# Adding the residual x to z with an accumulating DMA instead of GpSimd's additions

## What is computed

```python
y = jnp.einsum('bct,bcd->bdt', x, cond_w[condition])
z = jnp.einsum('bsd,od->bso', y, W) + b
u = jnp.einsum('bsd,edr->ebsr', y, A)
m = jnp.einsum('ebsr,ero,e->bso', u, B, p_scores)
gamma = jnp.minimum(0.5 * norm(z) / (norm(m) + 1e-6), 1.0)   # norms over the last axis
out = x + z + gamma * m
```

## Time and profile before

| | us |
|---|---|
| median of 3 runs | 942.87 |
| lowest and highest | 938.2 and 942.97 |
| the profiled execution: whole time | 940.29 |
| the profiled execution: span of instructions | 938.5 |
| granted clock of TensorE over the span | 0.990 of full speed |

### The profile page before, as it was taken

One profiled execution on the slowest core, in us unless ns is written; L12 is line 12 of the kernel. 1 busy time (PEld: TensorE's weight loads), 2 busy tenths in 40 slices (PEclk: granted clock), 3 DMA queues, 4 the chain that ended last, 5 costly groups with the idle time before them and its releaser, 6 DMA issues.

```text
span 938.5 us, 15150 instructions
## 1 busy us (share of the span) xinstructions
PE 914.9 (97%) x4884; PEld 789.7 (84%) x4884; DVE 576.1 (61%) x898; ACT 355.9 (38%) x694; POOL 317.9 (34%) x317
## 2 busy tenths in 40 slices
PE   6969999999999999999999999999999999999996
PEld 5858888888888888888888888888888888888885
DVE  4995555656555657555656555656556666556664
ACT  4443432433433443433343333343433343334342
POOL 0023323443323443224443224443224443224432
PEclk9989999999999999999999999999999999999999
DMA  7222112212112222122222122121122221122211
GB/s 258 84 75 89 47 70 92 92 70 92 45 71 92 87 75 86 42 78 92 78 84 78 41 87 92 70 92 69 46 92 92 70 92 65 50 92 92 71 46 67
DMA packets 32600, 75.16 MB, mean 80 GB/s; under 512 B 12745, under 2 KB 13770, under 8 KB 32586
## 3 DMA queue, kind: packets, MB, share of 16 engines
q1 hardware_dynamic: 32138, 74.43, 22.3%
q10 hardware_dynamic: 448, 0.56, 0.2%
HBM read 41.42 MB, written 33.55 MB: 80 GB/s over the span
## 4 chain that ended last, share of the span: by engine, by line
PE 95%; DVE 3%; ACTq 1%; DMA 1%; issue 1%; ACT 0%; DVEq 0%
PE b_ps L845 36%; PE c_ps L845 19%; PE mix_ps L832 12%; PE u_ps L884 9%; PE a_ps L845 9%; PE m_ps L895 9%; DVE w_lo L602 1%; ACTq L241 1%; DMA mixer<-in_L_cond_weights_dram 0%; PE m_ps L832 0%; DMA x_in<-in_x_dram 0%; PE m_ps L845 0%; DVE bias L761 0%; PE mix_ps L895 0%; DVE z L664 0%
## 5 line engine op out<-in xcount | busy, mean ns | idle before, releaser
L418 ACT CAST y_hi<-mix_ps 128x512 fp32r<-128x512 f32 x126 | 74.3, 591 | 315.5 <-PE mix_ps L832 315.5
L359 POOL TENSOR_TENSOR stats<-stats 128x1 f32<-128x1 f32 x32 | 18.7, 586 | 489.5 <-ACT squares L465 489.5
L632 DVE TENSOR_TENSOR s_lo<-s,s_hi 128x512 fp32r<-128x512 f32 x124 | 134.4, 1103 | 4.2
L832 PEld LDWEIGHTS mix_ps<-mixer,x_in 128*128 128x128 f32 x1008 | 123.6, 194 | 15.4 <-issue 10.6
L832 PE MATMUL mix_ps<-mixer,x_in 128*128 128x128 f32 x1008 | 124.4, 277 | 9.3 <-issue 8.2
L611 DVE TENSOR_TENSOR y_lo<-mix_ps,y_hi 128x512 fp32r<-128x512 f32 x126 | 86.5, 687 | 55.2 <-ACT s L424 44.4
L431 ACT CAST s_hi<-s 128x512 fp32r<-128x512 f32 x124 | 76.6, 618 | 114.2 <-POOL s L333 93.4
L345 POOL TENSOR_TENSOR z<-z,x_in 128x512 f32<-128x512 f32 x61 | 79.0, 1295 | 116.8 <-ACT squares L446 116.8
L845 PE MATMUL b_ps<-w_hi,y_hi 128*128 128x512 f32 x256 | 100.1, 391 | 0.0
L845 PE MATMUL b_ps<-w_lo,y_hi 128*128 128x512 f32 x256 | 100.0, 390 | 0.0
L845 PE MATMUL b_ps<-w_hi,y_lo 128*128 128x512 f32 x256 | 99.6, 389 | 0.0
(11 more groups left out here) (120 smaller groups left out, 1843.0 us busy)
## 6 DMA issues: line engine op xcount, KB each, us to landing
x_in<-in_x_dram SPq DMA_DIRECT2D x64, 512.0 KB, 3.6
out_dram<-z SPq DMA_DIRECT2D x63, 512.0 KB, 2.7
w_lo_raw<-in_L_ffn_W_dram SPq DMA_DIRECT2D x8, 256.0 KB, 6.4
mixer<-in_L_cond_weights_dram SPq DMA_DIRECT2D x126, 16.0 KB, 2.1
w_hi_raw<-in_L_ffn_W_dram SPq DMA_DIRECT2D x6, 256.0 KB, 6.2
w_hi_raw<-in_L_ffn_W_dram ACTq DMA_DIRECT2D x2, 256.0 KB, 4.3
a_lo_raw<-in_L_ffn_A_dram SPq DMA_DIRECT2D x1, 512.0 KB, 7.4
b_lo_raw<-in_L_ffn_B_dram SPq DMA_DIRECT2D x1, 512.0 KB, 6.9
```

What stands on the lines that cost most here:

```text
L359: nc.gpsimd.tensor_tensor(stat(NORM_Z, 1), stat(Z_SQ, 1), half, ALU.pow).then_inc(norm_z_ready[1], 1)
L418: nc.scalar.copy(y_part(y_hi, r, h), source(h)).then_inc(y_hi_ready, 1)
L632: nc.vector.tensor_tensor(s_lo[:, n, :, :], s_raw(n), s_hi[:, n, :, :].bitcast(fp32), ALU.subtract).then_inc(s_lo_ready, 1)
L832: made = nc.tensor.matmul(source(h)[:, k, :], x_in[:, slot, (h * HC + k) * P:(h * HC + k + 1) * P], mixer[:, r, :], start=True, stop=True)
```

## The change

For pairs 1 to 30, `residual1` and `residual0` no longer are additions of two tiles in SBUF. POOL issues a DMA that reads the tile of x once more from DRAM and adds it to z in SBUF as it writes, and DVE waits for the arrival of the transfer (`x_added`). SP's loads of later tiles of x no longer wait for the additions, except in the first step. The left half of z0 of pair 31 gets its addition on DVE, in the closing stretch. Pair 0 stays on DVE as it was.

```diff
+        x_added = [sem(f"x_added{r}") for r in range(2)]
...
                     if not closing:
-                        sp.wait_ge(residual1_ready, p)
+                        if first:
+                            sp.wait_ge(residual1_ready, 1)
                         sp.dma_start(x_in[:, 2 * (1 - j) + 1, :], x_tiles[2 * p + 3]
...
                     if not closing:
-                        sp.wait_ge(residual0_ready, 2 * p)
+                        if first:
+                            sp.wait_ge(residual0_ready, 2)
                         sp.dma_start(x_in[:, 2 * (1 - j), :], x_tiles[2 * p + 2]
...
-            def residual1(p, slot):
+            def residual1(p):
 
                 pool.wait_ge(z1_squared, p + 1)
-                nc.gpsimd.tensor_tensor(z1[:, :], z1[:, :], x_in[:, slot, :], ALU.add).then_inc(residual1_ready, 1)
-
-            def residual0(p, par, h):
-
-                cols = slice(h * H, (h + 1) * H)
-                pool.wait_ge(z12_squared if h else z11_squared, p + 1)
-                nc.gpsimd.tensor_tensor(z0[:, par, cols], z0[:, par, cols], x_in[:, 2 * par, cols],
-                                        ALU.add).then_inc(residual0_ready, 1)
+                nc.gpsimd.dma_start(z1[:, :], x_tiles[2 * p + 1], accum_op=ALU.add).then_inc(x_added[1], 16)
+
+            def residual0(p, par):
+
+                pool.wait_ge(z11_squared, p + 1)
+                pool.wait_ge(z12_squared, p + 1)
+                nc.gpsimd.dma_start(z0[:, par, :], x_tiles[2 * p], accum_op=ALU.add).then_inc(x_added[0], 16)
...
                         norm_z1(p - 1)
-                        residual1(p - 1, 2 * (1 - j) + 1)
+                        residual1(p - 1)
                         norm_m(p - 1, 1)
                         make_s1(p)
                         norm_z0(p - 1)
-                        residual0(p - 1, 1 - j, 1)
+                        residual0(p - 1, 1 - j)
                         make_s4(p)
                     if not opening:
-                        residual0(p, j, 0)
                         norm_m(p - 1, 0)
...
-            def add_m0(p, par):
+            def add_m0(p, par, first):
 
                 dve.wait_ge(gamma_ready[0], p + 1)
-                dve.wait_ge(residual0_ready, 2 * p + 2)
+                if first:
+                    dve.wait_ge(residual0_ready, 2)
+                else:
+                    dve.wait_ge(x_added[0], 16 * p)
...
-            def add_m1(p):
+            def add_m1(p, first=False):
 
                 dve.wait_ge(gamma_ready[1], p + 1)
-                dve.wait_ge(residual1_ready, p + 1)
+                if first:
+                    dve.wait_ge(residual1_ready, 1)
+                else:
+                    dve.wait_ge(x_added[1], 16 * p)
...
-            add_m1(PAIRS - 1)
+            dve.wait_ge(gamma_ready[1], PAIRS)
+            dve.wait_ge(residual1_ready, 2)
+            nc.vector.scalar_tensor_tensor(out=z1[:, :], in0=m_ps[:, :], scalar=stat(GAMMA, 1), in1=z1[:, :],
+                                           op0=ALU.mult, op1=ALU.add).then_inc(out1_ready, 1)
+            dve.wait_ge(z11_squared, PAIRS)
+            nc.vector.tensor_tensor(z0[:, 1, lo], z0[:, 1, lo], x_in[:, 2, lo], ALU.add).then_inc(residual0_ready, 1)
             dve.wait_ge(z12_squared, PAIRS)
```

More of the change, by code:

```diff
@@ L752, in _ @@
             make_gamma(0, 1)
-            add_m1(0)
+            add_m1(0, True)
             split_t(T2, 1)
@@ L792, in step @@
                     make_gamma(p - 1, 0)
-                    add_m0(p - 1, 1 - j)
+                    add_m0(p - 1, 1 - j, first)
                     split_u(p)
@@ L821, in _ @@
             dve.wait_ge(gamma_ready[0], PAIRS)
-            dve.wait_ge(residual0_ready, 2 * PAIRS)
+            dve.wait_ge(residual0_ready, 4)
             for c in (lo, up_):
```

## The result

| | before | after |
|---|---|---|
| median of 5 runs (two more of before than the prediction had), us | 942.25 | 949.96 |
| lowest and highest, us | 938.2 and 942.97 | 947.99 and 952.07 |
| profiled execution, whole time, us | 940.29 | 949.41 |
| its span, us | 938.5 | 947.7 |

The account below looks back on a forecast made before the run. PE was taken to bound the kernel, busy 97% of the span and without idle time in the pairs. 940.3 - 1.1 (opening) + 0.6 (end) + 27 (stalls behind z1's DMA) = 966.8, say 967 us; range 937 to 1030.

Parts of the forecast that it names:

- PE full, cover of 5.2 us: In the pairs PE has no idle time; z1's transfer may take 5.2 us from issue to landing before PE stalls.
- The landing, 6.1 us: z1's adding DMA lands 6.1 us after issue, midway between 5.4 and 6.9: 0.9 us stall in 30 pairs, 27 us.
- the doubled transfer: z1's DMA reads z and x: 1.0 us ahead, 2.2 us of movement and end doubled, landing 5.4 us.
- its forecast of no stall: The skill's rule for z1's DMA: 3.2 us for 512 KB, no surcharge for adding, 0 in place of 27 us.
- The estimate of 5.8 us: Landing of z1's DMA with the skill's later first byte added to doubled movement: 18 us in place of 27.
- B: Rival: z1's landing hidden, under 5.3 us, so not slower; 939.8 us, or 944 with a 0.15 us stall; chance 0.33.
- C: Rival: adding moves at a quarter of the pace, landing 9.8 us, stall 4.6 us per pair, 1078 us; chance 0.10.
- D: Rival: faster, opening gains over 1.1 us and DVE's splits get shorter, down to 935 us; chance 0.03.
- the forecast's own: Case of z1's DMA landing after 5.4 to 8.2 us, so slower, own range 945 to 1030 us; chance 0.54.
- z0's transfer costs nothing, SP's earlier loads cost nothing: In the pairs, z0's DMA has 10.7 us before add_m0 and SP's x loads go out earlier; cost 0 each.
- The opening, -1.1: Without POOL's addition beside it, DVE's L761 falls from 1.78 to 0.69 us; gain 1.1 us.
- The end, +0.6: Pair 31's left-half z0 addition, now on DVE's chain, costs 0.60 us.

Follow-up runs that it names:

- z1_late: The changed kernel with POOL issuing the DMA for z1 after norm_m(p-1, 1) instead of before it: 984.97 us, ratio to before 1.0472.
- z1_plain: The changed kernel with plain DMAs for z1 in place of adding ones, so x overwrites z1 (times only): 940.8 us, ratio to before 0.9992.
- z0_only: The changed kernel with z1 added by POOL again as before, and only z0 by the adding DMA: 939.43 us, ratio to before 0.9984.
- bias_first: The changed kernel with bias_p1(p) ahead of add_m1(p-1) in DVE's order: 940.54 us, ratio to before 0.9990.
- opening_only: The kernel before, no DMA added, with POOL's addition to the left half of pair 1's z0 moved later: 940.27 us, ratio 0.9987.
- bias_first_tail: The changed kernel with bias_p1 ahead of add_m1 on DVE and the last z0's left half added by POOL again: 939.75 us, ratio to before 0.9981.

## Why the prediction was wrong

The mechanism was right and one term of its sum was too large.

- **PE full, cover of 5.2 us.** Right. The cover turned out as 5.4 - 0.3 = 5.1 us. The slack was real to a tenth, and z1_late shows that beyond it each tenth costs a tenth per pair.
- **The landing, 6.1 us.** This is the step that failed; it was 5.4. The prediction had itself found 5.4 for the doubled transfer and called it "0.2 too late"; it then went to the middle between that and 6.9, the landing of a 512 KB load that queued with others in the opening. That row wasn't near (z1's transfer meets nothing but the last mixer load) and not the slowest of its kind either: the page of the kernel before has 7.4 and 7.7 us. By the parts, the prediction had 2.2 us for the doubling and 0.7 for the issue by POOL on top of SP's 3.2; measured are 1.7 for the adding (5.4 against 3.7) and 0.5 for POOL's path (3.7 against 3.2). Because only what exceeds 5.1 us counts, an error of 13% in the landing made the term 27 us in place of 10.1 (30 x 0.335).
- **Why 5.4.** That the doubled transfer came out at 5.4 was luck. Doubling holds for the time that the packets take, but the prediction's 1.0 us ahead and 4.4 of movement and end were 1.6 and 3.8: too little ahead, too much behind, and the errors cancelled. The Trainium skill's price (DMA: Bandwidth & Descriptors, "Anatomy of one DMA") of 3.2 us for 512 KB is nearer to the plain transfer (3.7) and misses the adding one by 2.2, so that its forecast of no stall failed. The estimate of 5.8 us, worked out from its later first byte, was closer than 6.1; the plain transfers agree with that later start (first packet after 1.3 us by POOL, 1.0 by SP).
- **The rivals.** B (hidden, landing under 5.3 us) missed by 0.1 us of landing; z1_plain, with 3.7 us, is what it had described. C (movement at a quarter of the pace) is out: the movement is 1.7 times as long. D's shorter splits came (L634, 1.89 us), and as it said they hit no wait of PE's. The case that came is the forecast's own, a landing of 5.4 to 8.2 us, at its lower end.
- **z0's transfer costs nothing, SP's earlier loads cost nothing.** Right, by z0_only for the transfer and by bias_first, which has both: no wait of PE's in the pairs, and 28.26 us per pair. With two adding transfers per pair the loads of x land after 4.3 us in place of 3.6, without anyone waiting.
- **The opening, -1.1.** The row is right: L761 is 1.09 us shorter. That the whole kernel gains it is likely and not shown: opening_only, which has nothing else, gives a ratio of 0.9987, and its interval reaches 1.
- **The end, +0.6.** Right by the rows: L830 takes 0.60 us on DVE's chain. bias_first_tail is 0.8 us below bias_first by the medians, which the intervals don't separate.
- **The sum** with the measured term: 940.3 - 1.1 + 0.6 + 10.1 = 949.9, against 949.41 in the profiled execution and a median of 949.96. That it meets them so closely is in part luck: the changes add up to +9.6 us, the runs differ by 8.6 (6.2 to 10.9), and the profiled execution that the sum starts from lies 2.0 us under the median of 942.25.

## What to carry to other kernels

Where one engine is full and another's work has slack, a slower way of doing that work is free up to the slack and costs its excess times the number of repetitions beyond it; so the sum needs the latency to a tenth of a microsecond near that point, and the forecast should stand on the row whose queue looks like the one in question, or else report the two sides of the threshold as open. Before a wait for a long transfer is accepted, look at what is queued behind it on the waiting engine: here a swap of two independent instructions on DVE took the loss away without making the transfer faster. An instruction moved ahead on an engine need not start earlier, so check where the time before it goes, and whether it goes the same way inside a loop and outside.

## What the runs showed of the hardware

- An adding DMA of 512 KB from DRAM to SBUF, issued by POOL, lands 5.4 us after its issue (5.2 to 5.7 in 30 of them), a plain one from the same place 3.7 (3.5 to 4.5). Its packets take twice the time (50.6 against 25.2 us, summed over the engines), and from the first to the last of them 3.5 against 2.0 us pass.
- The issue is recorded on POOL with 0.89 us (plain: 0.62), but POOL's next instruction starts 0.64 us after it in both (424.96 to 425.60 in the kernel after, 422.41 to 423.05 in z1_plain). With nothing between it and the wait ahead of it, it starts 0.66 us after the wait ends in the loop, where register instructions precede it, and 0.30 us in the unrolled steps.
- DVE's 128 x 512 addition of two SBUF operands took 1.78 us beside a POOL addition and 0.68 us without it. The three splits of a pair, which took 3.85 us beside POOL's reading, take 1.89 us in the kernel after (L634 at 403.62, above), where `make_s4` (L336, 401.33 + 1.60) has ended before they start. The Trainium skill (SBUF — State Buffer, "Who interferes with whom") states that a VectorE instruction with two SBUF inputs contends with a GpSimd instruction that reads SBUF; these rows agree. DVE is busy for 48 us less in the kernel after, and the pairs gain nothing by it; the opening, the one stretch where DVE and not PE was behind, likely gains the 1.1 us.
